# Skip term of twelve carried units: added on GpSimd instead of multiplied by the identity on TensorE, with the order of all blocks written anew

## Chip, cores and metric

One core of one Trainium2 chip. The metric is device time in microseconds (us) of one execution. The kernel before takes 487.6 us, the median of three runs (486.68 to 488.59).

## What is computed

A layer of three parts on four sequences of 512 tokens with 128 features: a Mamba-2 block (`attn_a`), a mixture of experts (`ffn`), an RWKV block (`attn_b`) and the experts again. Each part gets the layer-normalised sum so far and is added to it. Only the Mamba block is touched. Cut to that:

```python
q = apply_rope(q_part(x @ W_in.T))                     # residual = q
h = rmsnorm(q, norm_pre_w)
z, xBC, dt = split(h @ W_zxbcdt.T)
dt = softplus(dt + dt_bias)
xBC = silu(conv_b + sum(shift(xBC, k) * conv_w[:, k] for k in range(4)))
x_ssm, Bm, Cm = split(xBC)                             # 4 heads of 64, state of 128
A = -exp(A_log)
y = ssd(x_ssm, dt, A, Bm, Cm) + D_param * x_ssm        # D_param * x_ssm: the skip term
y = rmsnorm(y * silu(z), norm_gated_w)
return y @ W_out.T + residual
```

`ssd` is a scan over time. It is computed by chunks: inside a chunk the part `Y_diag` comes from the chunk's own tokens, and `Y_off` from the state that the chunks before have left, times a decay.

## The kernel before, in words

The program has two blocks. `phase_mamba` computes the Mamba block and `phase_body` all the rest. Each engine has its own program in a block, run strictly in order, and engines wait for each other by semaphores. At the end of `phase_mamba` all engines meet before `phase_body` starts. At the end of `phase_mamba`, TensorE already makes the first products of the experts (`first_unit`, L1195 to L1209).

The scan works on 16 units of 128 tokens. `units` lists them as (chunk c, sequence s): units 0, 1, 8 and 9 are the first chunks of a sequence (c = 0) and carry no state in; the other twelve (2 to 7 and 10 to 15) are the carried units. For a unit n:

- ScalarE makes `seg_l` (`segments`, GpSimd for four units in `segments_here`), TensorE sums it (`seg_sums`, L1120), ScalarE takes the exponential (`seg_exp`), VectorE masks the product of B and C (`masking`, L560) and multiplies both to `mix` (`mixing`, L567).
- GpSimd makes three products of the unit's tokens: `dx` = tokens by D (`skip_x`, L314, a ring of four), `xdt` = tokens by dt (`weigh_x`, L323) and `xw` (`decay_x`, L332).
- TensorE makes `Y_diag` in the left half of a PSUM bank (`within`): for a carried unit first the identity times `dx` (L1146), then on top of it four products of `mix` and `xdt`, one per head (L1151). It makes `Y_off` before its decay in the right half of the same bank (`carry`, L1137). All units up to 8 use one bank; from 9 on the odd ones have a second. Both `within` and `carry` wait until VectorE has read the last unit of that bank (`bank_of_y`).
- VectorE, in `joining`, waits for `within`, multiplies the right half by the decay into `y_off` (L593), waits for itself (`link`), and adds `y_off` and the left half into `y` (L599). For the units without a carried state it adds `dx` instead of `y_off`.
- GpSimd gates (`gating`, L341), ScalarE squares (`square_g`), GpSimd takes the power -1/2 (`rms_g`, L347), TensorE turns and projects (`turn_g`, `project_out`), VectorE closes the unit (`closing`, L608). VectorE also updates the state (`new_state`, L577 to L584) and ScalarE and TensorE turn and project around it; `add_state` is L1161.

Ahead of the units stand: layer norm of x on VectorE (`statistics`, `normalise`), with the power on GpSimd (`rsqrt_var`); turns and projection to q (`turn_x`, `project_q`); rotation on VectorE (`turn_q`, L515) and its sum on GpSimd (`add_q`, L279); squares on ScalarE (`square_q`) and the power on GpSimd (`rms_q`); the norm of the first sequence on VectorE (`rms_norm_first`, L504); the projection (`project_in`, L1064), the first tap of the convolution on ScalarE (`tap0`, L789), the other three on VectorE (`taps`, L524); and the step sizes: `dt_exp` and `dt_log` on ScalarE (each with another function table), `finish_dt` on VectorE (L543), for which `weigh_x` and `segments` wait. `split_high` (ScalarE) and `split_low` (VectorE) cut the experts' weights into two half-precision parts.

The order on each engine is written out by hand, as a list of calls at the end of each engine's program. These lists set what is queued behind what.

Of the kernel before, what the change touches and what calls it, by code (L numbers as in the profile page):

```python
# [111 lines left out]
def phase_mamba(core, io, shared):  # L112
# [22 lines left out]
    SEG_POOL = (1, 3, 5, 7)  # L135

    with ExitStack() as ctx:
# [65 lines left out]
        dt_made, dt_step, dt_act = sem("dt_made"), sem("dt_step"), sem("dt_act")  # L203
        segl_ready, segp_ready, dx_ready, xdt_ready, xw_ready = sem("segl"), sem("segp"), sem("dx"), sem("xdt"), sem("xw")
# [43 lines left out]
        def _(pool):  # L248
# [67 lines left out]

            def weigh_x(n):
# [53 lines left out]
            rsqrt_var(3)  # L371
            add_q(0, 0)
            add_q(0, 1)
            add_q(1, 0)
            add_q(1, 1)
            rms_q(0)
            rms_q(1)
            add_q(2, 0)
            gate_w_out(0)
            rms_norm(1)  # L380
            add_q(2, 1)
            add_q(3, 0)
            add_q(3, 1)
            rms_q(2)
# [3 lines left out]
            gate_w_out(1)  # L388
            add_residuals(0)
            add_residuals(1)  # L390
            skip_x(0)
            weigh_x(0)
            segments_here(1)
            add_residuals(2)
            add_residuals(3)
            skip_x(1)
            segments_here(3)
            weigh_x(1)
            weigh_x(2)
            gating(0)  # L400
            skip_x(2)
            skip_x(3)
            skip_x(4)
            decay_x(0)
            decay_x(1)
            gating(1)
            decay_x(2)
            rms_g(0)
            segments_here(5)
            decay_x(3)  # L410
            weigh_x(3)
            gating(2)
            weigh_x(4)
            rms_g(1)
            weigh_x(5)
            weigh_x(6)
            rms_g(2)
            segments_here(7)
            gating(3)
            skip_x(5)  # L420
            decay_x(4)
            decay_x(5)
            rms_g(3)
            weigh_x(7)
            gating(4)
            skip_x(6)
            skip_x(7)
            weigh_x(8)
            gating(5)
            skip_x(8)  # L430
            decay_x(8)
            rms_g(4)
            rms_g(5)
            gating(6)
            weigh_x(9)
            skip_x(9)
            weigh_x(10)
            decay_x(9)
            decay_x(10)
            decay_x(11)  # L440
            gating(7)
            rms_g(6)
            weigh_x(11)
            weigh_x(12)
            rms_g(7)
            gating(8)
            decay_x(12)
            skip_x(10)
            skip_x(11)
            skip_x(12)  # L450
            gating(9)
            rms_g(8)
            skip_x(13)
# [2039 lines left out]
```

## Time and profile before

| what | value |
|---|---|
| median of three runs | 487.6 us |
| the profiled execution | 487.41 us |
| its span | 485.6 us |
| `phase_mamba`, from the span's start to the first instruction of the next block | 122.97 us |
| `phase_body`, from there to the end | 362.63 us |
| busy over the span: TensorE, VectorE, ScalarE, GpSimd | 95%, 81%, 75%, 72% |

The 1.81 us between the execution and its span lie outside what the trace shows. Engines are named in the profile as PE (TensorE), PEld (its weight loads), DVE (VectorE), ACT (ScalarE), POOL (GpSimd) and SP. The ends of matrix products are modelled, so that of a run of them the distance between the starts is the time that one takes up. The products in single precision appear as two records each.

### The profile page before, as it was taken

Reading aid. Unit: us, or ns where it says so; the run is one execution under the profiler, and the core shown is the slowest. Engines: PE = TensorE matmul, PEld = TensorE weight load, DVE = VectorE, ACT = ScalarE, POOL = GpSimd, SP = SyncE. Lnnn points to the kernel's source line nnn. Section 1 sums busy time; section 2 is a strip of 40 time slices with the busy share of each in tenths; the row PEclk is TensorE's granted clock in tenths of the full one; section 3 lists DMA queues with packets and bytes.
Section 4 is the critical chain, followed back from the end, with each engine's and each line's share of the span. In section 5 each row is a group of like instructions: output and inputs, shape, how many; then the busy total and the mean of one; then the engine's idle time right before and its main releaser. Section 6 shows DMA issues by size and latency. Waiting matters only on the chain.

```text
span 485.6 us, 10621 instructions
## 1 busy us (share of the span) xinstructions
PE 461.7 (95%) x3690; PEld 322.0 (66%) x3690; DVE 393.0 (81%) x1056; ACT 365.2 (75%) x710; POOL 349.0 (72%) x401
## 2 busy tenths in 40 slices
PE   8898999999799999968999989999999999999996
PEld 7675789998466655536665747575657665766664
DVE  6889899788667868998899899979997867486765
ACT  2699999867777757945999669976897588767652
POOL 3673778878556596798788988698969683575652
PEclk9999999999999999998999999999999999999999
DMA  8111100101200000000000000000000000000000
GB/s 265 64 33 34 33 1 3 34 0 36 72 1 2 0 1 1 3 0 1 2 2 1 1 2 1 0 1 3 1 0 24 1 1 24 1 1 1 23 1 24
DMA packets 7061, 8.51 MB, mean 18 GB/s; under 512 B 608, under 2 KB 5216, under 8 KB 7008
## 3 DMA queue, kind: packets, MB, share of 16 engines
q1 hardware_dynamic: 7008, 7.83, 5.1%
q8 instruction: 30, 0.49, 0.4%
q14 instruction: 23, 0.19, 0.1%
HBM read 6.78 MB, written 1.05 MB: 16 GB/s over the span
## 4 chain that ended last, share of the span: by engine, by line
PE 46%; DVE 9%; POOL 8%; ACT 7%; issue 4%; DVEq 0%; ACTq 0%; POOLq 0%
PE bank L1601 8%; PE bank L1602 8%; PE bank L1605 8%; PE bank L1628 5%; PE bank L1630 5%; PE bank L1629 5%; DVE x L2010 2%; POOL b_hid_lo L2253 2%; DVE b_hid L1984 2%; PE bank L1729 1%; PE bank L1746 1%; ACT b_silu L1801 1%; PE bank L1671 1%; PE bank L1635 1%; ACT b_hid_hi L1808 1%
## 5 line engine op out<-in xcount | busy, mean ns | idle before, releaser
L2253 POOL TENSOR_TENSOR b_hid_lo<-b_hid,b_hid_hi 128x512 f16<-128x512 f32 x143 | 169.7, 1195 | 62.8 <-ACT b_hid_hi L1808 60.4
L1984 DVE SCALAR_TENSOR_TENSOR b_hid<-bank,b_silu 128x512 f32<-128x512 f32 x144 | 97.7, 686 | 38.2 <-ACT b_silu L1801 28.6
L1801 ACT ACTIVATE b_silu<-bank 128x512 f32<-128x512 f32 x144 | 85.5, 595 | 43.7 <-PE bank L1605 42.7
L1601 PE MATMUL bank<-x_hi,wsplit 128*128 128x512 f16 x284 | 108.0, 380 | 2.5 <-DVE b_hid L1984 1.7
L1628 PE MATMUL bank<-wsplit,b_hid_hi 128*128 128x128 f16 x576 | 101.2, 220 | 8.3 <-DVE x L2010 4.2
L1602 PE MATMUL bank<-x_hi,wsplit 128*128 128x512 f16 x284 | 107.8, 380 | 0.0
L1605 PE MATMUL bank<-x_lo,wsplit 128*128 128x512 f16 x284 | 107.6, 379 | 0.0
L1630 PE MATMUL bank<-wsplit,b_hid_lo 128*128 128x128 f16 x576 | 101.2, 220 | 0.0
L1629 PE MATMUL bank<-wsplit,b_hid_hi 128*128 128x128 f16 x576 | 101.2, 220 | 0.0
L1808 ACT CAST b_hid_hi<-b_hid 128x512 f16<-128x512 f32 x144 | 88.0, 611 | 13.4 <-DVE b_hid L1984 13.0
L2010 DVE SCALAR_TENSOR_TENSOR x<-bank,b_w_branch,x 128x128 f32<-128x128 f32 x256 | 71.6, 341 | 10.0 <-PE bank L1630 9.6
L1628 PEld LDWEIGHTS bank<-wsplit,b_hid_hi 128*128 128x128 f16 x576 | 56.7, 98 | 21.3 <-POOL b_hid_lo L2253 8.9
L1629 PEld LDWEIGHTS bank<-wsplit,b_hid_hi 128*128 128x128 f16 x576 | 56.7, 98 | 6.8 <-issue 1.3
L1630 PEld LDWEIGHTS bank<-wsplit,b_hid_lo 128*128 128x128 f16 x576 | 56.7, 99 | 0.0
L1605 PEld LDWEIGHTS bank<-x_lo,wsplit 128*128 128x128 f16 x284 | 27.8, 98 | 33.7 <-issue 0.3
L1601 PEld LDWEIGHTS bank<-x_hi,wsplit 128*128 128x128 f16 x284 | 28.5, 100 | 32.2 <-DVE b_hid L1984 5.8
L1602 PEld LDWEIGHTS bank<-x_hi,wsplit 128*128 128x128 f16 x284 | 27.8, 98 | 26.7 <-issue 5.3
L524 DVE SCALAR_TENSOR_TENSOR xbc<-bank,cols,xbc 128x511 f32<-128x511 f32 (+2 forms) x48 | 35.7, 746 | 2.3 <-ACT xbc L789 1.1
L1064 PE MATMUL bank<-normT,wzx 128*128 128x512 f32 x32 | 16.9, 610 | 1.6 <-DVE xbc L524 1.1
L1120 PE MATMUL bank<-causal,seg_l 128*128 128x128 f32 x128 | 17.2, 278 | 0.8 <-ACT seg_l L827 0.5
L1120 PEld LDWEIGHTS bank<-causal,seg_l 128*128 128x128 f32 x128 | 15.8, 191 | 2.7 <-issue 1.7
L1151 PEld LDWEIGHTS bank<-xdt,mix 128*128 128x128 f32 x128 | 16.4, 192 | 0.9 <-issue 0.3
(247 smaller groups left out, 926.8 us busy)
## 6 DMA issues: line engine op xcount, KB each, us to landing
moe_raw<-in_moe SPq DMA_DIRECT2D x9, 384.0 KB, 3.2
x<-in_x SPq DMA_DIRECT2D x4, 256.0 KB, 4.3
out<-x SPq DMA_DIRECT2D x3, 256.0 KB, 2.7
rope<-in_rope SPq DMA_DIRECT2D x1, 512.0 KB, 6.0
wzx<-in_wzx SPq DMA_DIRECT2D x1, 386.0 KB, 6.4
b_w_rkvo<-in_w_rkvo SPq DMA_DIRECT2D x1, 256.0 KB, 2.7
b_w_fk<-in_w_fk SPq DMA_DIRECT2D x1, 256.0 KB, 2.9
b_w_fv<-in_w_fv SPq DMA_DIRECT2D x1, 256.0 KB, 3.6
```

Of the source, the lines that this page charges most:

```text
L524: ins = nc.vector.scalar_tensor_tensor(xbc[:, b, t0 + back:t1], conv_ps[b % 2][:, 0:SEQ - back], col(core, "conv_w", TAPS * b + TAPS - 1 - ...
L1601: nc.tensor.matmul(dst, hi, x_hi[:, q % 2, :], start=True, stop=False)
L1602: nc.tensor.matmul(dst, lo, x_hi[:, q % 2, :], start=False, stop=False)
L1605: nc.tensor.matmul(dst, hi, x_lo[:, q % 2, :], start=False, stop=True).then_inc(made, 1)
L1628: nc.tensor.matmul(dst, h_hi, d_hi, start=blk == 0, stop=False)
L1629: nc.tensor.matmul(dst, h_hi, d_lo, start=False, stop=False)
L1630: ins = nc.tensor.matmul(dst, h_lo, d_hi, start=False, stop=blk == FBLK - 1)
L1801: nc.scalar.activation(silu[:, 2 * (u % 2) + blk, :], gate_ps[blk][:, :], ACT.Silu, scale=GU_UNSCALE).then_inc(silu_ready, 1)
L1808: nc.scalar.copy(hid_hi[:, FBLK * (u % 3) + blk, :], hid[:, 2 * (u % 2) + blk, :]).then_inc(hi_ready, 1)
L1984: nc.vector.scalar_tensor_tensor(hid[:, 2 * (u % 2) + blk, :], up_ps[blk][:, :], GU_UNSCALE * H_SCALE, silu[:, 2 * (u % 2) + blk, :], ALU. ...
L2010: ins = nc.vector.scalar_tensor_tensor(x[:, i, :], down_bank(u)[:, P * c:P * (c + 1)], w_branch[:, q % 2, e, c:c + 1], x[:, i, :], ALU.mul ...
L2253: nc.gpsimd.tensor_tensor(hid_lo[:, slot, :], hid[:, 2 * (u % 2) + blk, :], hid_hi[:, slot, :], ALU.subtract).then_inc(lo_ready, 1)
```

## The change

Twelve carried units are listed in `SKIP_ADDED`. For them:

- TensorE no longer makes the product of the identity and `dx`. The four products of `mix` and `xdt` start the left half themselves. `within` waits in its place for `off_ready`: VectorE must have read the right half.
- The decay of the right half (L593 before) is no longer made in `joining`, but in `carried_early`, a step of its own that stands earlier in VectorE's list.
- GpSimd adds `dx` to `y_off` in SBUF (`add_skip`), after `dx` and `off_ready`.
- `joining` waits for `skip_added` and adds `y_off` and the left half.

The lists of all four engines are written anew. The calls in them are the same but for `add_skip` (12 on GpSimd) and `carried_early` (12 on VectorE). The diff, its lists cut to the parts that are spoken of:

```diff
+    SKIP_ADDED = (2, 3, 4, 5, 6, 7, 10, 11, 12, 13, 14, 15)
...
+            def add_skip(n):
+                pool.wait_ge(dx_ready, n + 1)
+                pool.wait_ge(off_ready, SKIP_ADDED.index(n) + 1)
+                nc.gpsimd.tensor_tensor(y_off[:, n % 2, :], y_off[:, n % 2, :], dx[:, n % WRING, :],
+                                        ALU.add).then_inc(skip_added, 1)
...
+            def carried_part(n):
+                dve.wait_ge(carried, carried_no[n] + 1)
+                dve.wait_ge(dt_act, DECAYS)
+                return nc.vector.tensor_tensor(heads(y_off[:, n % 2, :]), heads(y_ps(n)[:, INNER:2 * INNER]),
+                                               per_head(decays[:, 0, tile_of(n), :]), ALU.mult)
+
+            def carried_early(n):
+                carried_part(n).then_inc(off_ready, 1)
+
             def joining(n):
                 c, s = units[n]
                 ps = y_ps(n)
                 dve.wait_ge(y_made, n + 1)
-                if c:
-                    dve.wait_ge(carried, carried_no[n] + 1)
-                    dve.wait_ge(dt_act, DECAYS)
-                    link(nc.vector.tensor_tensor(heads(y_off[:, n % 2, :]), heads(ps[:, INNER:2 * INNER]),
-                                                 per_head(decays[:, 0, tile_of(n), :]), ALU.mult))
+                if n in SKIP_ADDED:
+                    dve.wait_ge(skip_added, SKIP_ADDED.index(n) + 1)
+                elif c:
+                    link(carried_part(n))
...
-                if c:
+                by_product = c > 0 and n not in SKIP_ADDED
+                if by_product:
                     pe.wait_ge(dx_ready, n + 1)
                     nc.tensor.matmul(ps[:, 0:INNER], core.ident[:], dx[:, n % WRING, :], start=True, stop=False)
+                elif c:
+                    pe.wait_ge(off_ready, SKIP_ADDED.index(n) + 1)
...
-                                           start=c == 0, stop=c == 0 or h == HEADS - 1)
+                                           start=not by_product, stop=not by_product or h == HEADS - 1)
```

VectorE's list, at its head:

```diff
             normalise(0)
             statistics(2)
             normalise(1)
+            turn_q(0, 0)
+            turn_q(0, 1)
             statistics(3)
             normalise(2)
-            turn_q(0, 0)
-            turn_q(0, 1)
+            normalise(3)
+            rms_norm_first()
             turn_q(1, 0)
             turn_q(1, 1)
-            normalise(3)
             turn_q(2, 0)
-            rms_norm_first()
             split_low(0)
             turn_q(2, 1)
+            taps(0, 0)
             turn_q(3, 0)
-            split_low(1)
-            taps(0, 0)
...
             taps(1, 2)
+            finish_dt()
             taps(1, 3)
-            split_low(2)
-            finish_dt()
-            split_low(3)
             taps(2, 0)
```

The new lists around the carried units, as they stand after the change:

```
TensorE:  carry(2) turn_tok(6) products(4) within(2) add_state(2) carry(3) products(5) turn_g(1) seg_sums(4)
          project_in(3, 1) products(6) within(3) ... carry(4) seg_sums(6) project_in(3, 3) add_state(3)
          project_out(2) seg_sums(7) turn_tok(9) products(7) turn_g(3) turn_tok(10) within(4) seg_sums(8)
          add_state(4) carry(5) seg_sums(9) within(5) products(8) turn_tok(11) carry(6) project_out(3) within(6)
          ... carry(7) products(10) add_state(9) within(7) ... turn_g(12) carry(14) carry(15) turn_g(13)
          within(14) first_unit(0) within(15) project_out(12) project_out(13) turn_g(14) turn_g(15)
          project_out(14) project_out(15) first_unit(1)
VectorE:  ... joining(1) mixing(2) masking(3) carried_early(2) closing(0) new_state(1) masking(4) joining(2) ...
          closing(2) carried_early(4) taps(3, 3) joining(4) mixing(6) tile_stats(0) carried_early(5) ...
GpSimd:   ... gating(0) weigh_x(1) ... rms_g(0) gating(1) add_skip(2) skip_x(3) gating(2) skip_x(4) skip_x(5)
          add_skip(3) segments_here(5) ... weigh_x(7) add_skip(4) weigh_x(8) skip_x(7) skip_x(8) add_skip(5)
          gating(4) gating(5) add_skip(6) ...
ScalarE:  ... z_silu(4) conv_silu(1, 0, 2) dt_exp() tok_out(0) dt_log() tap0(1, 3) tap0(2, 0) segments(0)
          z_silu(5) ... split_high(8) load_silu() square_g(14) copy_gT(14) copy_gT(15) square_g(15)
```

In ScalarE's list before, `split_high(3)`, `tok_out(0)`, `tok_out(1)`, `z_silu(5)` and `tap0(1, 3)` stand ahead of `dt_exp`, and `load_silu` (a function table for the next block) is the last call. In TensorE's list before, `first_unit(0)` stands after `project_out(13)` and `first_unit(1)` ahead of `project_out(14)`.

## Rows read from the trace of the kernel before

**Rows 1.** Busy time by stage: TensorE, weight loads, VectorE, ScalarE, GpSimd, clock, DMA.

```profile
0.00:122.97 122.97, 115.66 (x738) 96.77 (x738) 103.03 (x252) 96.35 (x225) 82.57 (x130) 1.00 0.15 50
122.97:485.60 362.63, 346.03 (x2952) 225.20 (x2952) 289.93 (x804) 268.82 (x485) 266.43 (x271) 1.00 0.02 7
20.40:60.80 40.40, 37.24 (x202) 26.93 (x202) 34.74 (x58) 38.99 (x82) 24.93 (x36) 1.00 0.13 40
54.90:118.15 63.25, 63.04 (x470) 57.38 (x467) 54.86 (x132) 53.25 (x133) 50.45 (x77) 1.00 0.05 14
```

**Rows 2.** Timeline of TensorE around unit 2: start, length, line, operands, count.

```profile
61.56 0.59 PE L1146 MATMUL bank<-dx,ident 128*128 128x256 f32 x2
61.99 1.00 PE L1151 MATMUL bank<-xdt,mix 128*128 128x64 f32 x8
62.83 0.65 PE L1161 MATMUL bank<-xw,xtok 128*128 128x256 f32 x2
```

**Rows 3.** TensorE's products by line to 123 us: the identity's.

```profile
L1146 PE MATMUL bank<-dx,ident 128*128 128x256 f32 x24 | 7.3, 385 | 0.0
```

**Rows 4.** GpSimd's groups by line to 123 us: busy, mean ns, idle before.

```profile
L341 POOL TENSOR_TENSOR g<-y,sz 128x256 f32<-128x256 f32 x16 | 12.6, 790 | 4.9 <-PE bank L1175 3.7 <-DVE y L599 1.1
L314 POOL TENSOR_TENSOR dx<-xtok,cols 128x256 f32<-128x256 f32 x16 | 10.8, 687 | 3.4 <-ACT xtok L805 3.4
```

**Rows 5.** VectorE's groups by line to 123 us, of same columns.

```profile
L593 DVE TENSOR_TENSOR y_off<-bank,decays 128x256 f32<-128x256 f32 x12 | 5.0, 420 | 1.3 <-PE bank L1151 0.7 <-issue 0.4
L599 DVE TENSOR_TENSOR y<-y_off,bank 128x256 f32<-128x256 f32 x12 | 5.0, 420 | 0.4
L567 DVE TENSOR_TENSOR mix<-expo,gm 128x512 f32<-128x512 f32 x16 | 12.5, 780 | 2.2 <-ACT expo L834 1.5 <-issue 0.7
L553 DVE SCALAR_TENSOR_TENSOR wsplit<-moe_raw,wsplit 128x768 f16<-128x768 f32 x9 | 8.6, 973 | 0.0
```

**Rows 6.** Head of VectorE's timeline: rotations, first norm, first convolution.

```profile
10.81 0.86 DVE L487 BATCH_NORM_STATS2 stats<-x 128x6 f32<-128x128 f32 x4
13.22 1.41 DVE L515 TENSOR_TENSOR turned<-bank,rope 128x256 f32<-128x256 f32 x4
18.95 0.86 DVE L504 TENSOR_SCALAR norm<-q,rms 128x128 f32<-128x128 f32 x4
24.34 2.31 DVE L524 SCALAR_TENSOR_TENSOR xbc<-bank,cols,xbc 128x511 f32<-128x511 f32 x3
```

**Rows 7.** ScalarE's timeline: first tap, the exponential's table.

```profile
23.53 0.78 ACT L789 ACTIVATE xbc<-bank,cols 128x512 f32<-128x512 f32 x1 [0.32 <-PE bank L1064]
42.54 1.28 ACT L809 ACT_TABLE_LOAD   x1
```

**Rows 8.** GpSimd's timeline: the wait for the step sizes.

```profile
46.78 1.19 POOL L323 TENSOR_TENSOR xdt<-xtok,dt 128x256 f32<-128x256 f32 x1 [7.46 <-DVE adt L543]
```

**Rows 9.** VectorE's timeline: a short wait for TensorE; one slow mixing.

```profile
60.67 0.42 DVE L599 TENSOR_TENSOR y<-dx,bank 128x256 f32<-128x256 f32 x1 [0.16 <-PE bank L1151]
90.69 1.17 DVE L567 TENSOR_TENSOR mix<-expo,gm 128x512 f32<-128x512 f32 x1
```

**Rows 10.** GpSimd's timeline at that mixing.

```profile
90.59 0.72 POOL L341 TENSOR_TENSOR g<-y,sz 128x256 f32<-128x256 f32 x1
```

**Rows 11.** Source view of the mixings: shortest, median, longest ns.

```profile
L567 DVE TENSOR_TENSOR mix<-expo,gm x16: 680/684/1173, 53.9 to 115.1; 128x512 f32<-128x512 f32 x16
```

**Rows 12.** Timeline of all engines at the end of the first block.

```profile
117.20 1.11 PE L1183 MATMUL bank<-w_gated,gT 128*128 128x128 f32 x8
119.86 0.71 ACT L849 COPY gT<-bank 128x256 f32<-128x256 f32 x2 [0.23 <-PE bank L1175]
121.17 1.05 PE L1183 MATMUL bank<-w_gated,gT 128*128 128x128 f32 x8
121.89 0.80 DVE L608 SCALAR_TENSOR_TENSOR x<-bank,rms,q 128x128 f32<-128x128 f32 x2 [0.25 <-issue]
122.97 0.30 POOL L2367 MEMSET b_rank<- 128x1 f32 x8 [1.80 <-POOLq L137]
```

More of the change, by code:

```diff
@@ L692, in _ @@
-            mixing(4)
+            new_state(2)
+            mixing(3)
+            masking(5)
+            carried_early(3)
+            taps(3, 0)
+            mixing(4)
+            joining(3)
+            closing(1)
+            masking(6)
+            taps(3, 1)
+            taps(3, 2)
+            mixing(5)
             new_state(3)
-            taps(3, 2)
             closing(2)
-            mixing(5)
-            masking(6)
+            carried_early(4)
+            taps(3, 3)
             joining(4)
-            taps(3, 3)
+            mixing(6)
@@ L1292, in _ @@
-            turn_g(0)
-            project_in(3, 1)
-            within(2)
-            add_state(0)
-            seg_sums(4)
-            project_out(0)
-            products(4)
-            carry(2)
-            add_state(1)
+            products(4)
+            within(2)
+            add_state(2)
+            carry(3)
+            products(5)
+            turn_g(1)
+            seg_sums(4)
+            project_in(3, 1)
+            products(6)
+            within(3)
             turn_tok(7)
-            turn_g(1)
+            project_out(1)
@@ L1303, in _ @@
+            seg_sums(5)
+            turn_tok(8)
+            turn_g(2)
             project_in(3, 2)
-            add_state(2)
-            products(5)
-            project_out(1)
-            carry(3)
-            within(3)
-            turn_tok(8)
-            seg_sums(5)
-            turn_g(2)
-            add_state(3)
-            turn_tok(9)
+            carry(4)
             seg_sums(6)
             project_in(3, 3)
+            add_state(3)
             project_out(2)
-            within(4)
@@ L1318, in _ @@
-            products(6)
-            carry(4)
-            turn_tok(10)
-            seg_sums(7)
-            products(7)
+            seg_sums(7)
+            turn_tok(9)
+            products(7)
+            turn_g(3)
+            turn_tok(10)
+            within(4)
+            seg_sums(8)
+            add_state(4)
+            carry(5)
+            seg_sums(9)
             within(5)
-            carry(5)
+            products(8)
             turn_tok(11)
-            add_state(4)
-            seg_sums(8)
@@ L1344, in _ @@
+            products(10)
+            add_state(9)
+            within(7)
+            products(11)
+            seg_sums(10)
             project_out(5)
-            add_state(9)
-            seg_sums(10)
+            within(8)
+            within(9)
             turn_g(6)
-            within(8)
+            carry(10)
+            turn_tok(14)
+            seg_sums(11)
+            add_state(10)
             project_out(6)
-            within(9)
-            carry(10)
-            add_state(10)
+            within(10)
@@ L1382, in _ @@
             turn_g(11)
-            carry(14)
+            products(15)
             project_out(10)
             project_out(11)
+            seg_sums(15)
+            within(13)
+            turn_g(12)
+            carry(14)
             carry(15)
-            products(15)
-            seg_sums(15)
-            turn_g(12)
             turn_g(13)
             within(14)
+            first_unit(0)
             within(15)
@@ L1394, in _ @@
             project_out(13)
-            first_unit(0)
             turn_g(14)
             turn_g(15)
-            first_unit(1)
             project_out(14)
             project_out(15)
+            first_unit(1)
 class LayerNorm:
```

484 lines of the change are left out of this document (249 added, 235 removed).

## The prediction

> **What bounds the kernel now.** I read the busy times by stage first, then the timelines of the engines, then the groups by line. The span of 485.6 us falls into 122.97 us of `phase_mamba` and 362.63 us of `phase_body` [rows 1]. The change touches the first alone, and I take the second as it is. In the first there are two regimes. From about 20 to 61 us ScalarE is the full engine (38.99 of 40.40 us busy) and TensorE has gaps (37.24). From 54.90 us to the first product for the experts at 118.15 us TensorE is full: 63.04 of 63.25 us, at the full clock [rows 1]. The modelled ends could hide gaps there, so I added up the work of the stretch by distances between starts, as in [rows 2]; all its steps together need about 60.9 us, so some 2.4 us of 63.25 are waits in small pieces. There VectorE, ScalarE and GpSimd are busy 54.86, 53.25 and 50.45 us: none is the bound, but none has much to spare.
>
> **The products that go.** The identity's product starts at 61.56 and the next work at 61.99: it takes up 0.43 us (its mean of 380 ns is for each of two overlapping records) [rows 2, 3]. The 24 records are twelve products, all inside the full stretch: 12 x 0.43 = 5.2 us. The four products behind it keep their 0.84 us (61.99 to 62.83).
>
> **The additions that come.** The trace has no GpSimd addition of this form, but it has the gating, with the same shape and two inputs in SBUF: 0.79 us on average, and as the nearest from below `dx` with 0.69 us [rows 4]. I take 0.79: 12 x 0.79 = 9.5 us. In the full stretch GpSimd has 63.25 - 50.45 = 12.8 us free, of which 9.5 go to the additions and some 4 to the shorter stretch, if all else is the same. That is as good as nothing left, and so GpSimd's queue is where I look for losses. What hides an addition is the same unit's `within` on TensorE (0.84 us), which runs beside it. Uncovered, it would cost up to 0.79 us for each unit.
>
> **The work that moves.** VectorE's work is unchanged: 0.42 us for the decay and 0.42 us for the sum [rows 5]. The wait for itself between them goes (below 0.1 us each; I give it nothing). But `within` now stands behind `carried_early`, which stands behind `carry`: a hop to VectorE, 0.42 us, and a hop back. A hop from TensorE shows as 0.16 us of idle time [rows 9], so the loop needs about 0.42 + 2 x 0.16 = 0.74, say 0.8 us. What TensorE does between `carry` and `within` of a unit covers it: in steps of 0.22 to 0.88 us, which I read off the timeline, units 3, 4, 5, 10, 11, 12, 13 and 15 have 0.88 us or more; unit 2 has 0.55, unit 6 has 0.44, units 7 and 14 have 0.65. Short by 0.3, 0.4, 0.2 and 0.2 us: 1.1 us. This presumes that VectorE is free when `carry` ends. Behind a held `within` stand on TensorE `add_state`, the next `seg_sums` and the turns, and all engines wait for those. The bounds are 0 (VectorE comes early everywhere, or idle time elsewhere swallows it) and 12 x 0.8 = 9.6 us.
>
> **The shared inputs.** Some `mixing` steps take far longer than others: median 684 ns, mean 780 ns, longest 1173 ns [rows 5, 11]. The one at 90.69 us lasts 1.17 us beside a gating that began at 90.59 and ended at 91.31 [rows 9, 10]: 0.62 us of waiting and then little more than its usual time. Added up, the 16 mixings lose 16 x 0.096 = 1.5 us so, and the gatings and `dx` products, by their means against 0.72 and 0.61, another 2 us. Some 60 such GpSimd steps lose or cause about 4 us, 0.07 us each; twelve more make 0.8 us, which I charge in full (bounds: 0, and twelve full blocks of 0.68 us, 8 us). The Trainium skill, "SBUF — State Buffer", section "Who interferes with whom", says that a VectorE instruction with two SBUF inputs and a GpSimd instruction that reads SBUF exclude each other for a whole instruction; by that rule the trace agrees at 90.69 us, and the decay and the sum in `joining`, each with one input in PSUM, must stay at 0.42 us.
>
> **The head.** `turn_q` of the first sequence takes the place of the statistics at 10.81 us; it had begun at 13.22. Behind it hang sum, squares, power and first norm (18.95), which I put at about 15.7 to 16.5, and the first tap on ScalarE (23.53), at about 20.4 [rows 6, 7]. ScalarE has done about 1.2 us less by then, so that it is 1.9 us ahead. Ahead of `dt_exp` it has five calls fewer, 2.6 us: the table at 42.54 comes at about 38.0, and the step sizes, for which GpSimd had waited 7.46 us until 46.78 [rows 7, 8], at about 42.1. But VectorE does not have the work: `taps(1, 3)` (2.3 us) and two of the splits (0.97 us each), which stood ahead of the step sizes, now stand behind them [rows 5, 6]. Of 4.5 us about 0.4 survive on VectorE, 1.9 on ScalarE; TensorE, which needs both for the units, I give 1.2 us. Both ends are kept for the range. The number of ScalarE's table loads is the same by my count of the order of functions (eleven in the block).
>
> **The end.** Before, the two copies end at 120.57 and the last projections start at 121.17, since `first_unit(1)` fills the gap; they and the closings end at 122.69, and the next block starts at 122.97 [rows 12]. In the new list `first_unit(1)`, six products of 0.22 us, stands last and fills no gap: from the end of `within(15)` I count hop and sum 0.6, gating 0.8, turn 0.4, copy 0.45, projections 0.9, `first_unit(1)` 1.3 and meeting 0.3, which is 4.8 us to the next block, against 122.97 - 117.20 less the 1.3 us of `first_unit(0)`, which is 4.5. It costs 0.3 us. `load_silu` on ScalarE stands ahead of the last squares (1.28 us of table), but ScalarE has time to spare there.
>
> **The sum.** -5.2 (products) - 1.2 (head) + 1.1 (held `within`) + 0.8 (shared inputs) + 0.3 (end) = -4.2 us. The profiled execution took 487.41 us: 483.2 us. It lies 0.2 us below the median of 487.6, which is less than the three runs differ. A difference of about 0.5%, 2.4 us, is what a measurement of this kernel can tell from none; faster by that much means below 485.2 us.
>
> **The rivals.**
> (1) The waits eat the product. The additions sit in an in-order queue that is some 90% full; one that comes a GpSimd step late (0.69 us) holds `joining`, by that the only PSUM bank of the units up to 8, and by that the next `carry`. If it happens at half of the twelve, 6 x 0.5 = 3 us: -1.2 us, 486.2 us. For it: nearly no free time on GpSimd, new `add_skip` calls right ahead of `gating`. Against it: GpSimd's long wait at 46.78 falls away, and the lists put `add_skip` two or three calls ahead of its reader. Chance 0.18.
> (2) Slower: GpSimd becomes the bound. It decides from the point where a carried unit shows over 0.43 us of new idle time on TensorE. With both waits open, 0.42 + 0.79 us per unit against 0.43 gained: 12 x 0.78 = +9.4 us, less 1.2 of the head: 495.6 us; with half the units so, about 490. Its place is L599 waiting for GpSimd in the timeline. The Trainium skill, "GPSIMD Engine Reference", section "Engine selection", advises VectorE for elementwise work because GpSimd is about two times slower with two inputs; here the rows show 0.79 against 0.42 us, and it would hold if GpSimd's queue were on the path. Against it: three of the four engines are ahead of where they were when the units begin. Chance 0.10.
> (3) The head survives in full. If the 3.2 us of the first norm reached the units and nothing were held: -5.2 - 1.9 + 0.3 = -6.8 and less, 480.6 us and below. Against it: the engines in 20 to 60 us are full. Chance 0.07.
> (4) The product was free: had it been hidden behind weight loads (192 ns each), its going would give nothing and only the head would be left, 486 us or more. Against it: 0.43 us between starts. Chance 0.02.
>
> **How the numbers follow.** My forecast, 481 to 485.2 us, has the rest, 0.63. The bounds of the head (0.4 to 1.9) and of the held `within` (0 to 2.5, half the units at 0.4) set its width. To hold the time 8 times in 10 the range goes from 480.8 to 486.5 us, which takes in most of rival 1. Faster by over 0.5%: 0.63 + 0.07 and a little of rival 1, 0.72. Within 0.5%: 0.18. Slower: 0.10.
>
> **What would show it.** L1146 gone, and the five lines around it in the full stretch with the same distances. The full stretch from unit 2 on shorter by about 4 us. `phase_body` again 362.6 us. The step sizes near 42 us, with VectorE idle for some 2 us ahead of them. `add_skip` near 0.75 us, GpSimd over 90% busy from 60 us on. I am wrong if TensorE shows idle time ahead of L1151 of over 2.5 us in total, if VectorE waits for GpSimd ahead of L599, or if the units begin later than before.

## The result and the profile after

The changed kernel takes 488.98 us (median of 20 runs, 488.18 to 490.06) against 487.24 us for the kernel before (20 runs, 486.06 to 488.78). The ratio is 1.0034, with a 95% interval of 1.0025 to 1.0043: it is slower, by 1.7 us. The forecast was 483.2 us, and the range of 480.8 to 486.5 us does not hold the result. The profiled execution took 488.89 us, of which the span is 486.9 us.

Busy time by stage in the changed kernel, with the columns of [rows 1]: the first block, the second, and a late part of the units.

```profile
0.00:124.15 124.15, 112.72 (x714) 91.48 (x714) 102.72 (x252) 97.21 (x225) 92.70 (x142) 1.00 0.15 49
124.15:486.90 362.75, 346.08 (x2952) 225.19 (x2952) 290.03 (x804) 268.91 (x485) 266.83 (x271) 1.00 0.02 7
60.00:110.00 50.00, 47.60 (x341) 41.10 (x339) 43.62 (x109) 43.39 (x106) 46.76 (x68) 1.00 0.08 25
88.00:118.00 30.00, 27.83 (x211) 24.38 (x210) 23.91 (x65) 22.77 (x65) 29.11 (x42) 1.00 0.09 28
```

The second block is as long as before (362.75 against 362.63 us [rows 1]), so the loss lies in the first: 124.15 against 122.97. TensorE has the 24 records less (714 for 738) and is 2.94 us less busy, yet the block is 1.18 us longer. GpSimd has twelve instructions more and is busy 92.70 us instead of 82.57; from 88 to 118 us it has 0.9 us free in 30.

The groups of instructions of the changed kernel, as [rows 3 to 5] (busy, mean ns, idle time before them): the addition, the gating, the mixing, the decay, the final sum, the within products, and the turns of the gated output.

```profile
L322 POOL TENSOR_TENSOR y_off<-y_off,dx 128x256 f32<-128x256 f32 x12 | 8.7, 730 | 0.8 <-DVE y_off L609 0.8
L349 POOL TENSOR_TENSOR g<-y,sz 128x256 f32<-128x256 f32 x16 | 12.6, 787 | 2.3 <-DVE y L627 2.1
L587 DVE TENSOR_TENSOR mix<-expo,gm 128x512 f32<-128x512 f32 x16 | 12.9, 815 | 2.0 <-ACT expo L874 2.0
L609 DVE TENSOR_TENSOR y_off<-bank,decays 128x256 f32<-128x256 f32 x12 | 5.0, 417 | 0.8 <-PE bank L1177 0.7
L627 DVE TENSOR_TENSOR y<-y_off,bank 128x256 f32<-128x256 f32 x12 | 5.0, 418 | 6.2 <-PE bank L1194 3.6 <-issue 2.2 <-POOL y_off L322 0.3
L1194 PE MATMUL bank<-xdt,mix 128*128 128x64 f32 x128 | 16.1, 271 | 0.1
L1218 PE MATMUL bank<-ident,g 128*128 128x128 f32 x32 | 6.4, 282 | 2.7 <-DVE x L636 1.5 <-POOL g L349 0.8
```

Both new waits look harmless: TensorE is idle for 0.1 us ahead of `within` (L1194), and VectorE waits for the addition for 0.3 us in all (L627). TensorE's new idle time stands elsewhere: 2.7 us ahead of the turns (L1218), where `closing` of VectorE (L636) and the gating of GpSimd come late. In the kernel before these turns had 0.0.

For a ledger I added up TensorE's work by distances between starts, as the prediction did, from 20 us to the end of the first block. Each product counts with the median distance to the next start that its kind has in the kernel before, or with its own distance where that is shorter; what its distance has beyond it is idle time.

| us | ends | work | idle | of it from 60 us |
|---|---|---|---|---|
| before | 122.97 | 92.2 | 10.8 | 2.6 |
| after | 124.15 | 86.5 | 17.4 | 8.9 |

The work fell by 5.7 us; the idle time rose by 6.6, and 6.3 of that lie behind 60 us. (Another choice of the typical distance moves each number by some tenths, work and idle time in opposite ways.)

The head of the changed kernel, as [rows 6 to 8], on VectorE, ScalarE and GpSimd:

```profile
15.97 0.87 DVE L524 TENSOR_SCALAR norm<-q,rms 128x128 f32<-128x128 f32 x4
42.33 0.23 DVE L562 SCALAR_TENSOR_TENSOR dt<-dt_in,dt_exp 128x64 f32<-128x64 f32 x1 [1.44 <-ACT dt_exp L855]
38.72 1.28 ACT L849 ACT_TABLE_LOAD   x1
42.96 0.61 POOL L331 TENSOR_TENSOR xdt<-xtok,dt 128x256 f32<-128x256 f32 x1 [5.51 <-DVE adt L563]
51.36 1.04 POOL L371 TENSOR_TENSOR seg_l<-after,adt 128x512 f32<-128x512 f32 x1 [5.62 <-PE bank L1160]
79.07 0.41 DVE L627 TENSOR_TENSOR y<-y_off,bank 128x256 f32<-128x256 f32 x1
```

The first norm comes 2.98 us earlier, the table 3.8, the step sizes 3.8, and the sum of unit 0 1.85 (55.23 against 57.08). The lead is still there in the sums of units 2 and 3 (63.70 and 69.63 us, 2.75 and 1.84 ahead) and gone by unit 4, whose sum, at 77.53 us before, comes at 79.07. Three convolutions stand between the sums of units 3 and 4 in VectorE's new list, and one in the old, so a part of this is only another order of the same work.

### The profile page after: what moved, and what is told of

It reads as the page before. It is cut to its first block, busy times and chain, and to the rows that moved or that the text cites. A ratio compares the mean times of both kernels' runs of the same rounds, so it can differ in the third digit from the quotient of the medians.

```text
span 486.9 us, 10600 instructions
## 1 busy us (share of the span) xinstructions
PE 458.8 (94%) x3666; PEld 316.7 (65%) x3666; DVE 392.8 (81%) x1056; ACT 366.1 (75%) x710; POOL 359.5 (74%) x413
## 4 chain that ended last, share of the span: by engine, by line
PE 46%; DVE 9%; POOL 8%; ACT 7%; issue 4%; DVEq 0%; ACTq 0%; POOLq 0%
PE bank L1644 8%; PE bank L1645 8%; PE bank L1648 8%; PE bank L1671 5%; PE bank L1672 5%; PE bank L1673 5%; DVE x L2053 2%; POOL b_hid_lo L2296 2%; DVE b_hid L2027 2%; PE bank L1772 1%; PE bank L1789 1%; ACT b_silu L1844 1%; PE bank L1714 1%; PE bank L1678 1%; ACT b_hid_hi L1851 1%
## 5 line engine op out<-in xcount | busy, mean ns | idle before, releaser
L544 DVE SCALAR_TENSOR_TENSOR xbc<-bank,cols,xbc 128x511 f32<-128x511 f32 (+2 forms) x48 | 35.4, 746 | 2.6 <-ACT xbc L829 1.5
L1160 PE MATMUL bank<-causal,seg_l 128*128 128x128 f32 x128 | 17.2, 277 | 1.1 <-ACT expo L874 0.6
L1160 PEld LDWEIGHTS bank<-causal,seg_l 128*128 128x128 f32 x128 | 15.7, 192 | 1.8 <-issue 0.9
```

Source lines behind the costliest of these rows:

```text
L544: ins = nc.vector.scalar_tensor_tensor(xbc[:, b, t0 + back:t1], conv_ps[b % 2][:, 0:SEQ - back], col(core, "conv_w", TAPS * b + TAPS - 1 - ...
```

## The experiments

All times are medians of 4 to 20 runs, and each ratio is to runs of the kernel before on the same chip. Those have medians of 487.24 to 487.41 us. "Lists" are the written orders of the four engines in the first block.

**1. Take the change apart.** The lists alone, with before's code: the twelve products are made, and `add_skip` and `carried_early` are left out.

```diff
-            <the four lists of the kernel before>
+            <the four lists of the changed kernel, without add_skip(n) and carried_early(n)>
```

> The new lists with the old computation: the identity's products are back, no add_skip, and the decay is made in joining again. Theory Q (GpSimd's queue with twelve additions more is what the second half waits for): the lists are no harm by themselves and bring the head's 1 to 2.5 us, so 485 to 486.5 us, and GpSimd is busy under 85% from 88 to 118 us. Theory L (the new lists lose in the units, by closings and within steps that stand late; the additions cost little): slower than the changed kernel, since 5.2 us of products come back on TensorE, 491 us or more.

Measured: 494.34 us, ratio 1.0133 (1.0119 to 1.0148). The new order costs 7 us where the products are still made and the decay is back in `joining`; what is new beside it then brings 5.4 us. Here I took this for the price of the lists, to be added to the rest. Experiments 2 and 9 show that this is too simple.

**2. The changed kernel without the additions.** The final sum takes the decayed part as it is; the skip term of the twelve carried units is left out.

```diff
-            add_skip(2)
...
-                    dve.wait_ge(skip_added, SKIP_ADDED.index(n) + 1)
+                    dve.wait_ge(off_ready, SKIP_ADDED.index(n) + 1)
```

> The changed kernel without the twelve add_skip; joining waits for carried_early alone. The skip term of the twelve carried units is left out. Theory Q: the second half goes at TensorE's pace, 483 to 485 us, 4 to 6 us below the changed kernel. Theory L: the late calls stay, at most 1 us below it, 488 to 489 us.

Measured: 486.98 us, ratio 0.9988 (0.9976 to 1.0). The additions cost 2.0 us. And even without them, with the early head and no product, the kernel is only 0.3 to 0.6 us faster than before. The forecast of 483.2 us was out of reach before the first addition was made.

**3. The change without its lists.** Before's lists, and in them only what must move: `within` behind `carry`, `carried_early` a few calls ahead of `joining`, `add_skip` right ahead of `gating`.

```diff
-            within(4)
             products(6)
             carry(4)
+            within(4)
```

> The lists of before, with only what the change itself needs: add_skip right ahead of its gating, carried_early one or two calls ahead of its joining, within behind carry. Theory Q: GpSimd is as full as in the changed kernel and there is no head, so 489 to 492 us. Theory L: the products' 5.2 us come through, less 1 to 2 us of waits, 483 to 485 us. A third outcome, near 487 us, would say that the waits take what the product gave, with no queue full.

Measured: 519.25 us, ratio 1.0649 (1.0616 to 1.0681). The waits of that kernel (total, times, longest) and one stretch of its busy times:

```profile
PEld bank L1194 <- issue: 17.9, 11, 4.5
DVE y L627 <- POOL y_off L322: 12.6, 5, 4.2
PE bank L1194 <- DVE y_off L609: 5.4, 3, 4.1
75.00:88.00 13.00, 8.44 (x44) 7.13 (x44) 6.27 (x12) 5.62 (x16) 9.17 (x13) 0.78 0.00 1
```

Both waits of the change are open here, and they cost 32 us: far more than the sum of their hops, since everything queued behind a held instruction is held too. Idle for a third of the stretch, TensorE also shows a granted clock of 0.78 (0.82 from 88 to 100 us and 0.80 from 120 to 154), and what part of the 32 us is the clock's no run shows. The new lists, then, do what is needed of them: the chain of decay and addition is covered.

**4. The head.** The kernel before, with the first part of its four lists in the new order.

```diff
-            <lists up to within(1), weigh_decay(), seg_exp(3), gating(1)>
+            <the same calls in the new order>
```

> The kernel before; only the first part of each list, up to within(1), weigh_decay, seg_exp(3) and gating(1), is put in the new order. Both theories say that the head is a gain: step sizes at 42 to 43 us instead of 46.6, and 1 to 2.5 us of it kept to the end since TensorE is full behind it, 484.7 to 486.2 us. If ScalarE or VectorE take it back (their work is only moved), 487 us.

Measured: 489.6 us, ratio 1.0049 (1.003 to 1.0067). The sum of unit 0 comes at 54.93 us, 2.15 ahead, and that of unit 2 at 68.94, 2.5 behind. A part of it may be how the new head meets the old rest: ScalarE has one pair of table loads more (712 of its records for 710 in the whole), and from 60 to 75 us TensorE is granted 0.89 and is busy 13.44 of 15 us.

> As the run with the head alone, but z_silu(7) stands beside z_silu(6) again, so that ScalarE loads eleven function tables and not two more. If those loads were what turned the earlier head into a loss: 486 to 487 us, below the 489.6 of the head alone by 2.6 us or more. If the head's lead is lost in the splice for another reason, 489 us.

This moves `z_silu(7)` up to `z_silu(6)` to save the tables. Measured: 490.42 us (1.0037 to 1.0083). The loads stayed thirteen in the block, for eleven before, so the edit did not do what I meant, and what the head alone is worth with its tables in order stays open. Both runs show that its lead of 2 us at unit 0 is not carried on by itself: by unit 2 it is 1.8 us behind (68.21 against 66.45).

**5. The addition in the old order.** Before's lists; product gone; GpSimd adds `dx` to the finished sum in the call of the gating.

```diff
+                if units[n][0]:
+                    pool.wait_ge(dx_ready, n + 1)
+                    link(nc.gpsimd.tensor_tensor(y[:, n % 2, :], y[:, n % 2, :], dx[:, n % WRING, :], ALU.add))
                 nc.gpsimd.tensor_tensor(g[:, n % 2, 0:INNER], y[:, n % 2, :], sz[:, tile_of(n), :],
...
-                if c:
-                    pe.wait_ge(dx_ready, n + 1)
-                    nc.tensor.matmul(ps[:, 0:INNER], core.ident[:], dx[:, n % WRING, :], start=True, stop=False)
```

> The kernel before with its own lists; the product with the identity is gone for the twelve units, and GpSimd adds dx to y after joining, right ahead of the gating, so that no engine gets a new wait ahead of within. Theory W (the product's 5.2 us are real, and the changed kernel loses them to the lists that the new waits need): TensorE's work falls by 5.2 us, the addition costs 0.7 us of delay for each unit in front of a chain that has slack, 483 to 485 us. Theory Q (GpSimd's twelve additions are the loss by themselves): 486.5 us or more, GpSimd over 95% busy from 88 us on.

Measured: 495.2 us, ratio 1.0168 (1.0142 to 1.0193), and with the new head on top:

> Both of the last two. If the gains add up: the late addition's time plus what the fixed head gives against the kernel before, 482 to 485 us. If they don't, no better than the late addition alone.

498.74 us (1.0201 to 1.0253). Busy times in the first of the two:

```profile
75.00:88.00 13.00, 12.16 (x91) 10.90 (x91) 11.73 (x31) 11.70 (x25) 12.77 (x19) 1.00 0.01 3
88.00:100.00 12.00, 10.05 (x81) 9.39 (x79) 8.25 (x16) 8.68 (x28) 11.92 (x18) 1.00 0.11 33
```

Of the five busy times of each row GpSimd's is the last and TensorE's the first: GpSimd is full in both stretches, and in the second TensorE has 2 us of idle time. Up to unit 7 this kernel was ahead of before, by up to 1.1 us; from unit 8 on it is behind.

**6. The slip at unit 4.** Three convolutions stand ahead of `joining(4)` in the new list of VectorE. Two of them are moved: `taps(3, 2)` behind `carried_early(4)`, still ahead of the sum, and only `taps(3, 3)` behind the sum:

```diff
-            taps(3, 2)
...
             carried_early(4)
+            taps(3, 2)
+            joining(4)
             taps(3, 3)
-            joining(4)
```

> The changed kernel with two convolutions moved on VectorE: taps(3, 2) behind new_state(3), closing(2) and carried_early(4), and taps(3, 3) behind joining(4) instead of ahead of it. If the first slip of the units (joining of unit 4 at 79.07 instead of 77.53 us) comes from the three convolutions ahead of it and is carried to the end: 486.5 to 487.5 us. If the slip is made up or replaced later, 488.5 to 489.5 us as the changed kernel.

Measured: 493.63 us, ratio 1.0121 (1.0089 to 1.0152), and unit 4 still ends at 79.17. The convolutions are wanted by then: TensorE waits 1.6 us for one (L1160 for L544), and the granted clock falls to 0.87 from 75 to 88 us. So moving one convolution out of the way does not bring unit 4 forward, and my reason for this run is not borne out. Two convolutions still stand ahead of that sum, so the run does not rule out that they hold it.

**7. Half of the units.** The changed kernel with six products back, either those of units 10 to 15 or those of 2 to 7.

```diff
-    SKIP_ADDED = (2, 3, 4, 5, 6, 7, 10, 11, 12, 13, 14, 15)
+    SKIP_ADDED = (2, 3, 4, 5, 6, 7)
```

> The changed kernel with the skip term of units 10 to 15 back on TensorE (six products with the identity, six fewer additions and early decays); units 2 to 7 as changed. The lists alone gave 494.3 us with all twelve products and 489.0 with none, so twelve are worth 5.4 us. Theory L (the products are worth the same in both halves, and the loss is in the order of the lists): half of it, 491.6 us, within 490.9 to 492.4, with the six products back as 6 x 0.45 us of TensorE work behind 88 us. Theory Q (GpSimd's queue behind 88 us, 97% busy, gives the late additions' worth away): the late half brings nothing, 489.0 us or less, and GpSimd is busy 24 to 25 us of the 30 between 88 and 118 us instead of 29.1.

> The other half: units 2 to 7 have their product back, units 10 to 15 are as changed. Theory L: 491.6 us, within 490.9 to 492.4. Theory Q, in which the first half carries all of the gain: 494 us or more. With the run before it this says where the 5.4 us come from: the two halves must add up to it if they don't touch each other (the sum of both times is then 983.3 us).

Measured: 491.55 us (1.0064 to 1.0093) and 491.50 us (1.0069 to 1.0096). The halves add up: 491.55 + 491.50 = 983.05, and the lists alone and the changed kernel make 494.34 + 488.98 = 983.32. So no part of the units carries the gain or the loss alone, although GpSimd is 97% full from 88 to 118 us, with the second half, and 91% from 60 to 88. That the halves weigh the same is less sure: in the profiled executions the first block ends at 125.91 us with the products of units 10 to 15 back and at 127.74 with those of units 2 to 7, for 124.15 with none. In both runs the decay of the units with a product is back in `joining` too.

**8. The end.** The changed kernel with `first_unit(1)` ahead of the last projections and `load_silu` last, as before.

```diff
+            first_unit(1)
             project_out(14)
             project_out(15)
-            first_unit(1)
```

> The changed kernel with the end of its lists as before: the second projection of the first expert unit ahead of the last output projections, and the table load behind the last square. My forecast charged 0.3 us for the new end. If that holds, 488.7 us and a gap of 4.5 us from the end of the last within to the start of the next block instead of 4.8; the rival is that the end costs nothing, 489.0 us. The 7 us of the lists do not lie here: they would if the time fell below 486 us.

Measured: 489.54 us (489.14 to 490.04), 0.6 us more than the changed kernel, with ranges that overlap. In its profile the last sum starts at 119.86 us and the next block at 125.24, 5.4 us later; in the changed kernel it is 119.51 and 124.15, 4.6 us. The new end is the better one, if it makes any difference.

**9. The product by itself.** The kernel before, its lists untouched, the twelve products left out and nothing put in their place; the skip term of the carried units is not added.

```diff
-                if c:
-                    pe.wait_ge(dx_ready, n + 1)
-                    nc.tensor.matmul(ps[:, 0:INNER], core.ident[:], dx[:, n % WRING, :], start=True, stop=False)
```

> The kernel before with its own lists, the twelve products with the identity left out and nothing put in their place: the skip term of the carried units is not added at all. It shows what TensorE's product is worth by itself where no list is touched and no wait is new. By my term of the sum, 12 x 0.43: 487.2 - 5.2 = 482.0 us. Rival 1, that the order of before hides part of it since other engines are nearly full there (GpSimd busy 11.4 of 13 us in 75 to 88): 484 to 486 us, with new idle time on TensorE ahead of within and seg_sums. Rival 2, that TensorE's chain held up more than its own work: below 481 us.

Measured: 486.4 us (485.29 to 487.55), ratio 0.9978 (0.9964 to 0.9992). This is the run that decides the case. The term that I put at -5.2 us is worth -1.1 us by the ratio (-0.9 by the medians), with no new wait and no list touched. In the profiled execution the block ends at 120.90 us, 2.07 earlier. Runs of both kernels beside each other that have the same mean granted clock, 0.996, give 1.0: a median span of 484.4 us (7 runs) for 485.4 (3 runs). So the worth lies between 1 and 2 us. Stretches and waits of this kernel:

```profile
60.00:110.00 50.00, 48.58 (x357) 43.11 (x356) 45.11 (x111) 42.87 (x108) 41.25 (x62) 1.00 0.06 17
PE bank L1148 <- DVE mix L567: 1.2, 3, 0.5
PEld bank L1148 <- DVE y L599: 1.1, 2, 0.9
81.24 1.08 PE L1148 MATMUL bank<-xdt,mix 128*128 128x64 f32 x8 [0.52 <-DVE mix L567]
82.57 0.67 PE L1137 MATMUL bank<-state,xbc 128*128 128x256 f32 x2 [0.25 <-DVE state L581]
```

In the kernel before TensorE is busy 49.96 us of the same 50. Here it has gaps, and those shown end with VectorE: a mixing, a sum that frees the bank, a state. VectorE is busy 45.11 of the 50 us, more than the other two. By the ledger TensorE's work is 86.8 us for 92.2, and its idle time 14.0 for 10.8. Of 5.3 us taken away 3.2 come back as waiting. That VectorE is the limit is read from these waits; no run made VectorE's work less.

**10. The product twice.** Still open were why TensorE, full as it is, gives so little, and which side of the addition costs the 2.0 us.

```diff
+                    nc.tensor.matmul(ps[:, 0:INNER], core.ident[:], dx[:, n % WRING, :], start=True, stop=True)
                     nc.tensor.matmul(ps[:, 0:INNER], core.ident[:], dx[:, n % WRING, :], start=True, stop=False)
```

> The kernel before with the product with the identity made twice in each of the twelve carried units (the second overwrites the first): 12 x 0.45 us more for TensorE, nothing moved, no new wait. Theory B: TensorE is a full bound of the units, busy without a gap from 60 us on, and only with the product gone do the other engines limit as well. Then more work costs its whole price, 487.3 + 5.2 = 492.5 us, within 491.6 to 493.2, though less work gave 1.1 us. Theory C: the product is mostly covered in the order of before (as the 1.1 us for leaving it out might say): 488.5 us or less.

Measured: 492.05 us (491.04 to 492.32), ratio 1.0089 (1.0072 to 1.0105): 4.7 us more than the before runs beside it, 0.39 us for each product. Upward TensorE is the full bound; its ledger is 97.1 us of work and 10.4 of idle time. Downward it is not.

**11. Additions that nobody waits for.** In the old order, product kept, each carried unit's gating is preceded by an addition of two other tiles into one that is read no more:

```diff
+                if units[n][0]:
+                    pool.wait_ge(z_done, 1)
+                    nc.gpsimd.tensor_tensor(turned[:, n // 2 % 2, n % 2, :], sz[:, 0, :], sz[:, 1, :], ALU.add)
```

> The kernel before, product kept, with one more GpSimd addition in each of the twelve carried units, 128 x 256 with both inputs in SBUF, ahead of the wait of that unit's gating, into a tile that nobody reads: it takes time in GpSimd's queue and nothing waits for it. GpSimd has 12.8 us free in 53 to 118 us and gets 12 x 0.73 = 8.8 us more. If free time is cover: 487.3 to 488.0 us. If the queue's place in the order counts (a gating behind each of them): 12 x 0.3 to 0.6 us, 491 to 494 us. The run with the addition on the path in the same place and no product gave 495.2 us, 8.8 above the kernel with neither; near that, the cost is the queue's time and not the addition's place on the path.

Measured: 490.77 us (490.21 to 491.3), ratio 1.0066 (1.0051 to 1.0081). They cost 3.4 us. The same additions in the place of `add_skip` in the changed kernel, whose final sum then waits for the decay alone; the skip term of the carried units is left out:

```diff
-                pool.wait_ge(dx_ready, n + 1)
-                pool.wait_ge(off_ready, SKIP_ADDED.index(n) + 1)
-                nc.gpsimd.tensor_tensor(y_off[:, n % 2, :], y_off[:, n % 2, :], dx[:, n % WRING, :],
-                                        ALU.add).then_inc(skip_added, 1)
+                pool.wait_ge(z_done, 1)
+                nc.gpsimd.tensor_tensor(turned[:, n // 2 % 2, n % 2, :], sz[:, 0, :], sz[:, 1, :], ALU.add)
```

> The changed kernel, its twelve additions kept in their places in GpSimd's list, but adding two other tiles into one that nobody reads, without the wait for the decayed part; the final sum waits for the decay alone. The skip term of the carried units is left out. The kernel without additions gave 487.0 us, the changed one 489.0. If the 2.0 us are the time in GpSimd's queue: 489.0 us (within 488.5 to 489.3). If they are the waits that the addition makes (for the decay, and of the sum for it): 487.0 us (486.6 to 487.6).

Measured: 488.94 us (488.62 to 491.11), ratio 1.0041 (1.0026 to 1.0055). The changed kernel has 488.98. GpSimd of the old order with idle additions (two stretches and their group), then that group in the new order:

```profile
75.00:88.00 13.00, 12.87 (x96) 11.78 (x95) 11.29 (x26) 12.00 (x25) 13.00 (x20) 1.00 0.01 3
88.00:100.00 12.00, 11.52 (x93) 10.83 (x92) 9.50 (x24) 9.87 (x30) 12.00 (x18) 1.00 0.12 34
L338 POOL TENSOR_TENSOR turned<-sz 128x256 f32<-128x256 f32 x12 | 9.6, 799 | 0.1
```

```profile
L321 POOL TENSOR_TENSOR turned<-sz 128x256 f32<-128x256 f32 x12 | 8.9, 747 | 0.0
```

An addition that nobody waits for costs as much as the real one. So the 2.0 us are not the two waits that it makes, but its presence on GpSimd. That has two sides, and these runs do not separate them: the time in the queue, in front of gatings and weighings, and what an addition does to the steps of VectorE beside it. The mixings without additions, then with idle ones, both in the new order:

```profile
L575 DVE TENSOR_TENSOR mix<-expo,gm 128x512 f32<-128x512 f32 x16 | 11.6, 733 | 2.0 <-ACT expo L862 2.0
L585 DVE TENSOR_TENSOR mix<-expo,gm 128x512 f32<-128x512 f32 x16 | 14.0, 888 | 2.0 <-ACT expo L872 2.0
```

The changed kernel has 815 ns. The first block of the five kernels in their profiled executions, and VectorE's busy time in it (us):

| | first block | VectorE |
|---|---|---|
| kernel before | 122.97 | 103.03 |
| before, with idle additions | 126.10 | 106.72 |
| changed, without additions | 122.13 | 101.34 |
| changed kernel | 124.15 | 102.72 |
| changed, with idle additions | 124.48 | 104.59 |

VectorE has the same 252 instructions in each, and 1.4 to 3.7 us more to do with additions on GpSimd than without. The blocks do not grow in step with it (3.25 us more on VectorE cost 2.35, 1.38 more cost 2.02), so it is hardly the whole cost; how much of it is VectorE's stays open.

All that matters, in one table (us):

| | lists of before | new lists |
|---|---|---|
| product | 487.24 | 494.34 |
| neither | 486.40 | 486.98 |
| product and idle additions | 490.77 | |
| idle additions | | 488.94 |
| additions | 519.25 (waits open), 495.2 (at the gating) | 488.98 |

The change is the way from 487.24 to 488.98: without the product 486.40 (-0.8), in the new order with its early decay 486.98 (+0.6), and with the additions 2.0 more, +1.7 in all. Each order without product is near 486.5 to 487 us, which fits that other engines limit there. In the new lists the product costs 7.4 us (494.34 - 486.98), more than its own 5.2. That run also has the decay back in `joining`, so the 7.4 are not the product's alone; that these lists suit only a kernel without it is likely, but not shown.

## Why the prediction was wrong, point by point

**The products, -5.2 us: this is the step that failed.** The cost itself was read rightly (0.43 us each by the start distances [rows 2, 3]; 5.7 us less work in the ledger after, 0.39 us for each product added in experiment 10). What failed is that it entered the sum in full. The prediction itself said that VectorE, ScalarE and GpSimd were busy 54.86, 53.25 and 50.45 of 63.25 us, "none is the bound, but none has much to spare" [rows 1], and then asked only of GpSimd what would be late next. Experiment 9 gives -1.1 us in its place, and its waits name VectorE as what is late next. A wait of 2.4 us in small pieces, which the prediction had found in that stretch, may have been the sign that TensorE was already handed its work just in time. The three signs of being wrong hardly catch this: the idle time ahead of `within` is 0.1 us, VectorE waits only 0.3 us for the additions, and the units begin earlier.

**The additions.** 0.73 us each (12 x 0.79 forecast, 8.7 us in all). That GpSimd would have nothing left was right (over 90% from 60 us on: 46.76 of 50, 29.11 of 30). The price was not: I charged 0.8 us for them under the shared inputs, and they cost 2.0. Rival 2, GpSimd as the bound, and rival 1, the waits, looked for the loss in L599 (now L627) waiting for GpSimd; that wait is 0.3 us. Experiment 11 shows what neither of them had: an addition costs without being waited for, by its time in the queue, by what it takes from VectorE, or by both. The "Engine selection" advice of the Trainium skill ("GPSIMD Engine Reference") is to make such sums on VectorE; no run here made these on VectorE, so whether that would be better is not shown. That section has a factor of about two for operations with two inputs; in this trace it is 0.73 to 0.42 us, 1.7, VectorE having one of its inputs in PSUM.

**The held `within`, +1.1 us.** It cost next to nothing that shows: 0.1 us of idle time ahead of L1194 on TensorE. Experiment 3 shows that this is owed to the order: without cover the two waits together cost 32 us, where the bounds were 9.6 us here and 9.4 in rival 2. No run in the new order takes the wait for the decay itself away, so its price in the 0.6 us between 486.40 and 486.98 is not known.

**The shared inputs, +0.8 us.** The mixings went from 780 to 815 ns (16 x 0.035 = 0.6 us), but that compares two orders. In the new order they have 733 ns without the additions and 815 with them, 1.3 us in all, and VectorE as a whole has 1.4 us more: the size was too small where the additions alone are looked at. The two steps with one input in PSUM stayed at 0.42 us, as forecast, and the gatings did not change (790, 787).

**The head, -1.2 us.** Every forecast time came within 0.8 us (first norm 15.97, table 38.72 for 38.0, step sizes 42.33 for 42.1), and VectorE was idle 1.44 us ahead of them. Unit 0 is 1.85 us early. But the new lists without product end no earlier than the old ones without it (486.98 and 486.40), so none of it reaches the end. Why it is spent, between units 3 and 4 by the sums, stays open: experiment 4 had more table loads, and experiment 6 did not find the cause.

**The end, +0.3 us.** Its sign was probably wrong: put back, it is 0.6 us slower, which may be nothing. The last projections of the changed kernel and what follows them, to set beside [rows 12]:

```profile
120.34 0.95 PE L1218 MATMUL bank<-ident,g 128*128 128x128 f32 x4 [0.49 <-DVE x L636]
121.21 1.25 PE L1226 MATMUL bank<-w_gated,gT 128*128 128x128 f32 x8
122.30 0.38 PE L1250 MATMUL bank<-x_hi,wsplit 128*128 128x512 f16 x1
124.15 0.30 POOL L2410 MEMSET b_rank<- 128x1 f32 x8 [1.27 <-POOLq L138]
```

`first_unit(1)` now runs beside the last closings and beside GpSimd's last powers (the meeting wait is 1.27 for 1.80 us), which my count had in a row.

**The rivals.** The result, 488.98 us, lies between rival 1 (486.2) and rival 2 (490 to 495.6). Rival 2's point of decision, 0.43 us of new idle time for each carried unit, was passed: 6.6 / 12 = 0.55 us by the ledger. Rival 4, "the product was free", had 0.02, and only for the reason that weight loads might hide it; leaving the product out gave little for another reason, and this is the case that was missing.

## What to carry to other kernels

An engine that is busy without a gap set the price of more work here, and not of less: adding the product cost 4.7 us, leaving it out gave 1.1. Before a product is taken off a full engine, ask of every other engine how much earlier it could deliver, and count the gain only up to the first that can't. Work moved to an engine whose in-order queue is nearly full is paid for even where nobody waits for it; an idle operation in the same place measures this in one run, together with what it takes from the engine beside it.

## What the runs showed of the hardware

The second block, which no run touches, took 361.57 to 363.80 us in the profiled executions, in steps of about 1.1 us. The granted clock about 93 to 102 us behind the start of that block goes with it. The kernel before (362.63 us), the one without products (363.80) and the one with the product twice (361.61), in this order, each from 93 to 96 us and from 96 to 102 us behind the start of its own second block:

```profile
215.97:218.97 3.00, 0.84 (x4) 0.20 (x2) 2.73 (x3) 0.00 (x0) 2.76 (x5) 1.00 0.00 0
218.97:224.97 6.00, 4.73 (x35) 3.80 (x36) 4.47 (x8) 4.56 (x10) 6.00 (x7) 0.72 0.00 0
```

```profile
213.90:216.90 3.00, 0.85 (x4) 0.19 (x2) 2.71 (x3) 0.00 (x0) 2.76 (x5) 1.00 0.00 0
216.90:222.90 6.00, 4.71 (x30) 3.34 (x31) 4.50 (x8) 4.28 (x10) 6.00 (x7) 0.52 0.00 0
```

```profile
220.49:223.49 3.00, 0.87 (x5) 0.19 (x2) 2.70 (x3) 0.00 (x0) 2.75 (x5) 1.00 0.00 0
223.49:229.49 6.00, 4.69 (x44) 3.48 (x45) 5.32 (x10) 4.94 (x11) 6.00 (x7) 1.00 0.01 3
```

The same quiet stretch, in which TensorE is busy for 0.84 to 0.87 of 3 us, is followed by a fall from 2.4 towards 1.2 GHz in some executions and by none in others, and this makes up to 2.2 us that have nothing to do with the change: more than the change itself. This is why medians of several runs decide here, and a single profile only shows where. The clock falls in the units as well where waits are opened: experiment 3 shows 0.78 to 0.82 in three stretches, 4 and 6 show 0.89 and 0.87 in one each, and the kernels before and after 1.00 over the whole block.
